# Five scan buffers, single absolute-value buffers and new due times in a one-core Mamba, attention and feed-forward block

## The reference

```python
x = x + selective_scan(layernorm(x))      # 16 states, scan over the 512 tokens
x = x + ffn(layernorm(x))                 # fp4-quantised, 256 -> 704 -> 256, gate and up
x = x + linear_attention(layernorm(x))    # 16 heads of 16, running sums over tokens
x = x + ffn(layernorm(x))                 # the same feed-forward again
```

## Time and profile before

| what | value |
|---|---|
| median of 3 runs | 3002.07 us (3000.82 to 3004.05) |
| the profiled execution: its time | 3002.07 us |
| its span in the profile | 3000.3 us |
| mean granted clock of TensorE | 0.921 |
| busy: PE, DVE, ACT, POOL | 82%, 79%, 63%, 32% |
| instructions | 40700 |

### The profile page before, as it was taken

One profiled execution on the slowest core, in us unless ns is written; L12 is line 12 of the kernel. 1 busy time (PEld: TensorE's weight loads), 2 busy tenths in 40 slices (PEclk: granted clock), 3 DMA queues, 4 the chain that ended last, 5 costly groups with the idle time before them and its releaser, 6 DMA issues.

```text
span 3000.3 us, 40700 instructions
## 1 busy us (share of the span) xinstructions
PE 2453.8 (82%) x12908; PEld 1396.4 (47%) x12908; DVE 2364.2 (79%) x4136; ACT 1900.8 (63%) x3677; POOL 963.7 (32%) x1632
## 2 busy tenths in 40 slices
PE   3559798887979788797988879798887979879796
PEld 1115354453535445354554535455353545536464
DVE  7776887969788796978879697887969788787744
ACT  4667667585766757576575757658575675846342
POOL 3012332333333232333333233233323323333432
PEclk7669899999999999999999999999999999989898
DMA  3321212112121211212112121211212121121000
GB/s 74 109 81 53 70 44 72 47 53 67 49 71 46 64 55 47 74 41 78 41 52 73 40 76 43 75 46 52 73 40 75 45 74 46 52 60 40 4 5 9
DMA packets 104434, 165.97 MB, mean 55 GB/s; under 512 B 15442, under 2 KB 34078, under 8 KB 104222
## 3 DMA queue, kind: packets, MB, share of 16 engines
q1 hardware_dynamic: 104222, 163.37, 19.8%
HBM read 146.55 MB, written 16.78 MB: 54 GB/s over the span
## 4 chain that ended last, share of the span: by engine, by line
PE 40%; DVE 36%; ACT 17%; issue 5%; POOL 2%; DMA 1%; SPq 0%; DVEq 0%; ACTq 0%; POOLq 0%
PE bank L916 10%; PE bank L899 9%; DVE scan_bufs L1187 7%; DVE scan_bufs L1197 4%; PE acc_y L864 4%; PE bank L956 3%; DVE rounding L1055 2%; ACT p_xT L615 2%; DVE f_h_max L1082 2%; ACT masked_scores L667 2%; PE bank L896 2%; PE bank L937 2%; DVE f_h L1057 2%; PE bank L909 1%; ACT scan_bufs L605 1%
## 5 line engine op out<-in xcount | busy, mean ns | idle before, releaser
L1187 DVE TENSOR_TENSOR_SCAN scan_bufs<-scan_bufs,inp_bank 128x512 f32<-128x512 f32 x512 | 617.2, 1205 | 24.4 <-ACT scan_bufs L607 12.9
L899 PE MATMUL bank<-w_gu,f_xqT 128*128 128x512 f32 x1024 | 495.8, 629 | 52.1 <-ACT f_xqT L667 23.6
L916 PE MATMUL bank<-w_dn,f_hqT 128*128 128x256 f32 (+1 forms) x1536 | 425.7, 423 | 36.3 <-ACT yT L667 33.6
L864 PE MATMUL acc_y<-scan_bufs,sel_y 128*32 128x512 f32 x1024 | 301.1, 674 | 127.9 <-DVE scan_bufs L1197 127.8
L605 ACT ACTIVATE scan_bufs<-scan_bufs,a_rows 128x512 f32<-128x512 f32 x512 | 365.4, 714 | 9.2 <-DMA scan_bufs<-dt_copy 8.7
L916 PEld LDWEIGHTS bank<-w_dn,f_hqT 128*128 128x128 f32 (+1 forms) x1536 | 297.0, 207 | 155.9 <-issue 78.9
L1197 DVE TENSOR_TENSOR scan_bufs<-scan_bufs,c_bank 128x512 f32<-128x512 f32 x512 | 343.6, 671 | 11.8 <-issue 0.2
L899 PEld LDWEIGHTS bank<-w_gu,f_xqT 128*128 128x128 f32 x1024 | 197.3, 201 | 310.0 <-issue 263.9
L607 ACT ACTIVATE scan_bufs<-scan_bufs 128x512 f32<-128x512 f32 x512 | 322.6, 630 | 16.2
L527 POOL TENSOR_TENSOR f_h<-f_h,f_h_inv 128x704 f32<-128x704 f32 x128 | 178.2, 1392 | 368.0 <-DVE f_h_inv L1086 368.0
L527 POOL TENSOR_TENSOR f_h<-f_h,f_h_scale 128x704 f32<-128x704 f32 x128 | 178.3, 1393 | 278.2 <-DVE f_h L1057 278.1
(11 more groups left out here) (194 smaller groups left out, 4642.7 us busy)
## 6 DMA issues: line engine op xcount, KB each, us to landing
scan_bufs<-dt_copy SPq DMA_DIRECT2D x512, 256.0 KB, 3.6
xp<-L_attn_a_x SPq DMA_DIRECT2D x16, 512.0 KB, 4.1
dt_copy<-dt SPq DMA_DIRECT2D x32, 256.0 KB, 2.0
out<-x SPq DMA_DIRECT2D x64, 128.0 KB, 2.0
w_attn<-L_attn_b_W_attn SPq DMA_DIRECT2D x1, 768.0 KB
scan_bufs<-L_ffn_w_gate SPq DMA_DIRECT2D x1, 704.0 KB
scan_bufs<-L_ffn_w_up SPq DMA_DIRECT2D x1, 704.0 KB
masked_scores<-L_ffn_w_down SPq DMA_DIRECT2D x1, 704.0 KB
```

What stands on the lines that cost most here:

```text
L864: last = nc.tensor.matmul(acc_y[32 * j:32 * j + 32, :], sel_y[:, q, :], bar[slot][:, h, :], start=(q == 0), stop=(q == 3), tile_position=( ...
L899: last = nc.tensor.matmul(to[:, :], f.xqT[:, k, :], w_gu[:, k, g, lo:hi], start=(k == 0), stop=(k == DH - 1))
L916: last = nc.tensor.matmul(to[:, 0:D], f.hqT[0:n, k, :], w_dn[0:n, k, :], start=(k == 0), stop=(k == FK - 1))
L1187: nc.vector.tensor_tensor_scan(half, half, inp[:, :], 0.0, ALU.mult, ALU.add)\
```

## The change

It adds a fifth slot to `scan_bufs`. It gives each feed-forward one buffer in place of two for the absolute values of x and of h, and ACT therefore waits for the rounding of the tile before in place of the one two tiles before. And it changes many of the beats in `TIMES`, and one in `PARTS_AT`.

```diff
-SLOTS = 4
+SLOTS = 5
...
-"S": (48.95, 16, 2), "Y": (65.0, 1, 2)
+"S": (48.75, 16, 2), "Y": (65, 1, 2)
...
     "sp": {
-        ("P", "load"): 2.25, ("P", "keep0"): 24.5, ("P", "keep1"): 26.7, ("D", "spread"): -3.55, ("R2", "down"): 13.9,
+        ("P", "load"): 1.35, ("P", "keep0"): 24.4, ("P", "keep1"): 26.6, ("D", "spread"): -3.05, ("R2", "down"): 14.8,
...
     "pe": {
-        ("P", "xT0"): 7.35, ("P", "xT1"): 10.1, ("P", "u0"): 10.3, ("P", "u1"): 14.6, ("P", "low"): 15.4,
-        ("P", "B"): 16.6, ("P", "C"): 32.6, ("P", "dt0"): 20.5, ("P", "dt1"): 24.5, ("P", "G"): 30.6,
+        ("P", "xT0"): 7.35, ("P", "xT1"): 8.3, ("P", "u0"): 10.5, ("P", "u1"): 14.55, ("P", "low"): 15.4,
+        ("P", "B"): 16.6, ("P", "C"): 32.4, ("P", "dt0"): 20.5, ("P", "dt1"): 23.5, ("P", "G"): 30.6,
...
-        ("R1", "a_s0"): 16.2, ("R1", "a_s1"): 17.35, ("R1", "a_sum"): 18.3, ("R1", "a_flip"): 18.8,
-        ("R1", "a_turn_y"): 20.3, ("R1", "a_proj"): 21.0, ("R2", "turn_x"): 5.0, ("R2", "up0"): 5.8,
-        ("R2", "up1"): 7.7, ("R2", "turn_h"): 10.7, ("R2", "down"): 11.6,
+        ("R1", "a_s0"): 16.2, ("R1", "a_s1"): 17.35, ("R1", "a_sum"): 18.1, ("R1", "a_flip"): 18.8,
+        ("R1", "a_turn_y"): 20.3, ("R1", "a_proj"): 21.0, ("R2", "turn_x"): 5.3, ("R2", "up0"): 5.8,
+        ("R2", "up1"): 7.8, ("R2", "turn_h"): 10.7, ("R2", "down"): 12.3,
...
-                self.x_abs = [sb(f"{name}_x_abs{i}", [P, D], BF16) for i in range(2)]
-                self.h_abs = [sb(f"{name}_h_abs{i}", [P, F], BF16) for i in range(2)]
+                self.x_abs = sb(f"{name}_x_abs", [P, D], BF16)
+                self.h_abs = sb(f"{name}_h_abs", [P, F], BF16)
...
-                    if not first(b, t - 1):
-                        act.wait_ge(f.x_rounded, upto(b, TILES, t - 2))
-                    nc.scalar.activation(f.x_abs[r][:, :], f.x[r][:, :], ACT.Abs, scale=ROUNDER_PER)\
+                    if not first(b, t):
+                        act.wait_ge(f.x_rounded, upto(b, TILES, t - 1))
+                    nc.scalar.activation(f.x_abs[:, :], f.x[r][:, :], ACT.Abs, scale=ROUNDER_PER)\
```

More of the change, by code:

```diff
@@ L33 @@
 BEATS = 2 * NS
-SLOTS = 4
+SLOTS = 5
 HALVES = NS * DH
 N_SETUP_POOL = 26
-PARTS_AT = {"P": (0, 0, 1), "M": (32, 1, 32), "D": (32, 2, 16), "G": (32, 2, 16), "S": (48.95, 16, 2), "Y": (65.0, 1, 2), "R1": (66, 3, 4), "R2": (95.7, 7, 4)}
+PARTS_AT = {"P": (0, 0, 1), "M": (32, 1, 32), "D": (32, 2, 16), "G": (32, 2, 16), "S": (48.75, 16, 2), "Y": (65, 1, 2), "R1": (66, 3, 4), "R2": (95.7, 7, 4)}
 LAST_AT = {"R1": (66, 3), "R2": (88, 3)}
@@ L688, in ffn @@
                     act.wait_ge(f.h_scaled, upto(b, TILES, t))
-                    if not first(b, t - 1):
-                        act.wait_ge(f.h_rounded, upto(b, TILES, t - 2))
-                    nc.scalar.activation(f.h_abs[r][:, :], f.h[r][:, :], ACT.Abs, scale=ROUNDER_PER)\
+                    if not first(b, t):
+                        act.wait_ge(f.h_rounded, upto(b, TILES, t - 1))
+                    nc.scalar.activation(f.h_abs[:, :], f.h[r][:, :], ACT.Abs, scale=ROUNDER_PER)\
                         .then_inc(f.abs_ready[1], 1)
@@ L1225, in ffn @@
                     dve.wait_ge(f.abs_ready[0], upto(b, TILES, t))
-                    round_mag(ch, (f.x[r][:, :], rounding[:, 0:D]), f.x_abs[r][:, :], f.x_rounded, b, t)
+                    round_mag(ch, (f.x[r][:, :], rounding[:, 0:D]), f.x_abs[:, :], f.x_rounded, b, t)
                 elif s in ("up0", "up1"):
@@ L1255, in ffn @@
                     dve.wait_ge(f.abs_ready[1], upto(b, TILES, t))
-                    round_mag(ch, (f.h[r][:, :], rounding[:, :]), f.h_abs[r][:, :], f.h_rounded, b, t)
+                    round_mag(ch, (f.h[r][:, :], rounding[:, :]), f.h_abs[:, :], f.h_rounded, b, t)
             def attention(b, par, t, s):
```

## The result

The changed kernel takes 3073.86 us, the median of 4 runs (3072.65 to 3074.98), against 3001.45 us for the kernel before beside it: ratio 1.0241, 95% interval 1.0223 to 1.0259. It is slower, as forecast, but by 72 us and not by 42, and outside the range. The profiled execution has a span of 3072.1 us.

What follows compares the result with a forecast made beforehand. No engine is full; the interlocking of the engines' hand-written orders bounds the kernel, delays of the leading engine being paid in full. 3002.1 + 42.9 (13 batches) + 4.4 (tail) - 5 (slot) = 3044.4 us; range 3000 to 3070.

Steps and rivals of the forecast that it cites:

- Steps 1 to 6: Six reorderings in one batch, from its boundary to a_qkv of tile 2: +0.65, +0.8, 2.3 (including both), -0.7, +0.2, +1.2 us.
- the norm: ScalarE does P norm ahead of the tanh of R2 up0, so VectorE gets the tanh later: +0.8 us a batch.
- turn_h ahead of u0: TensorE does R2 turn_h before P u0 and resumes 2.5 us later, of which 2.3 a batch are let through.
- a_sum ahead: a_sum of tiles 0, 1 and 2 goes before a_qkv of the next tile: 0.2 + 1.2 + 0.3 us a batch.
- 2.3 - 0.7 + 0.2 + 1.2 + 0.3 = 3.3 us: Whole batch: late turn_h, R1 up1 and turn_h of tile 2 earlier, then three a_sum moves; 42.9 us for 13 batches.
- step 7: a_sum of tile 2 before a_qkv of tile 3, R2 down of tile 2 behind dt1 on VectorE: +0.3 us, between 0 and 0.9.
- the short third kind of batch: One batch in three keeps the full clock at u0; none expected to afterwards, 0.6 us on average, in the high end only.
- The tail: Last stage, R2 of the last batch: TensorE's up0 ahead of down delays VectorE on three tiles, +4.4 us in all.
- The slot: Fifth scan-buffer slot removes ScalarE's wait for copies in the first batch: -5 us, between 0 and 6.5.
- A: Rival: the moves are hidden in VectorE's 32 us without work per batch; time 3002 us, chance 0.08.
- C: Rival: the single absolute-value buffer binds in the feed-forwards, 52 us on top of the forecast; time 3096 us, chance 0.04.
- B: Rival: R1 down of tile 3 keeps the full clock, gaining 2.25 us a batch; time 2973 us, chance 0.16.

Runs made afterwards that it cites:

- d1: Kernel before with one needless addition on VectorE per batch, 0.77 us longer: ratio 1.0050, batch 177.5 us.
- d3: Kernel before with two needless additions on VectorE per batch, 1.55 us longer: ratio 1.0109, batch 178.5 us, in threes.
- d2: Kernel before with three needless additions on VectorE per batch, 2.47 us longer: ratio 1.0212, batch 180.6 us.
- h1_fill: Kernel before with needless TensorE products in three waits (ahead of P u0, a_turn_y of tile 0, a_turn of tile 2): ratio 1.0201, batch 180.6 us.
- g4_fill: Kernel before with needless TensorE products in four waits, those of h1_fill and a_flip of tile 1: ratio 0.9982, batch 175.7 us.
- h2_fill: Changed kernel with needless TensorE products in seven long waits: ratio to the kernel before 1.0182, batch 179.7 us.
- e4_down: Kernel before with only R2 down later and the C projection ahead of it: ratio 1.0034, batch 177.5 us.
- e3_asum: Kernel before with only a_sum of a tile ahead of a_qkv of the next: ratio 1.0074, batch 177.5 us.
- e5: Kernel before with only R2 turn_h of tile 0 ahead of P u0 on TensorE: ratio 1.0047, batch 177.6 us.
- e1: Kernel before with five scan slots and single absolute-value buffers, all beats as before: ratio 1.0000, batch 176.5 us.
- e2: Changed kernel's beats with the old four scan slots and double absolute-value buffers: ratio to the kernel before 1.0242, batch 181.0 us.
- g5_fill: Kernel before with needless TensorE products in five waits, those of g4_fill and R2 turn_x of tile 0: ratio 0.9981, batch 175.9 us.
- f34_two_undone: Changed kernel with the a_sum moves and the R2 down and C moves undone: ratio to the kernel before 1.0345, batch 184.3 us.

## Why the prediction was right in direction and wrong in size

- **Steps 1 to 6 as places**: right, within 0.3 us in the changed trace, up to the last logarithm, 2.95 late for a predicted 3.0. As prices of a whole batch they were not: the norm alone costs 0.2, turn_h ahead of u0 alone 1.2, a_sum ahead alone 1.1 in place of 1.7.
- **The step that failed** is the sum: "2.3 - 0.7 + 0.2 + 1.2 + 0.3 = 3.3 us", added to a batch of 176.4 with the clock left as it was. The measured 4.9 close as 2.95 up to the logarithm, 1.1 behind it (step 7, next point), 0.45 for the short third kind of batch, which is gone (the batch read here was one of 176.85, the mean was 176.4), and 0.4 for two long batches. Of the 1.6 missed, 0.8 are step 7, 0.45 the short batch, which I had written down as 0.6 and put into the range and not into the sum, and 0.4 the long ones. The premise that a delay in the leading engine "is paid in full", and no more, fell too: a pure delay costs 1.4 to 1.7 times itself (d1, d3, d2). Two parts of that are shown: the short third batch goes with the smallest delay, 0.4 us of the 1.1, and low stretches grow, the one at u0 to twice its length with 2.47 us, 1.2 us.
- **Step 7**, "something between 0 and 0.9; I take 0.3": it measured 1.1 in this batch (2.95 late at the logarithm, 4.05 at the batch's end against 176.85 us), counted from last read to last read; from first scan to first scan 0.5 of the loss lies behind the logarithm. The stretch at 1.2 GHz from 1552 to 1562 falls on it: R2 down of tile 2 takes 5.17 us, and a_qkv of tile 3, now also behind a_sum of tile 2, starts 155.45 us behind the last read, before at 146.11. h1_fill against g4_fill shows that such a stretch, some 10 us earlier in the order, costs up to 4.9 us, and h2_fill's own batches that it costs some 3 us there. In the changed kernel itself its share of the 1.1 stays open: e4_down, with only 3.41 us at 1.2 GHz there, takes 28.5 us behind the logarithm too.
- **The batches together**: 63.4 us for 42.9: 4.5 a batch in the steady state, 0.4 on average from the two long batches, whose cause I did not find. "13 equal batches" was misread to begin with: those of the kernel before come in threes.
- **The tail**: +4.4 for a measured +8.2 behind the last scan, and +4.8 between the last batch's first and last scan, which my sum left out altogether: 13.0 together. The exchange itself was sized about right, though misread: PE does up0 of a tile ahead of the down of the tile two before, and for two tiles, not three. DVE's last three L1237 lie 19.17 and 16.78 us apart, before 15.78 and 14.73, 5.4 us more for my 4.4, and 1.2 come back behind them. The other 8.9 of the 13.0 us lie ahead, between the last batch's first scan and the first of these three, and my sum had nothing for them. e3_asum alone is 10.5 us late there, so they go with a_sum ahead of a_qkv in the last batch; e4_down is 3.6 early there. In e3_asum PE waits twice for q_par, 3.5 us together, ahead of the scores, which it did not before; that a_sum no longer stands between a_qkv and the scores would explain it, and the rest of the 10 us was not traced.
- **The slot**: the start came out at -4.8 for my -5 by luck. 4.0 come with the beats alone; the buffers alone are worth 2.4 there and nothing in the time.
- **Rivals**: A (hidden) and C (single buffer) are refuted, by e3 to e5 and by e1 and e2. B fell: R1 down of tile 3 kept its low clock (5.34 us), and g5_fill shows that with every low stretch gone a batch is 1.4 us shorter, not 2.25.

The changed tail's last two tiles on DVE, then the last of the kernel before, whose 2957.39 is in the earlier trace rows:

```profile
3028.36 0.69 DVE L1237 SCALAR_TENSOR_TENSOR f_h<-f_tanh,bank 128x512 f32<-128x512 f32 x1 [0.21 <-DVE x L1215]
...
3044.50 0.42 DVE L1215 TENSOR_TENSOR x<-bank,x 128x256 f32<-128x256 f32 x1 [4.46 <-PE bank L916]
3045.14 0.69 DVE L1237 SCALAR_TENSOR_TENSOR f_h<-f_tanh,bank 128x512 f32<-128x512 f32 x1 [0.21 <-DVE x L1215]
```

```profile
2972.12 0.69 DVE L1237 SCALAR_TENSOR_TENSOR f_h<-f_tanh,bank 128x512 f32<-128x512 f32 x1 [2.00 <-ACT f_tanh L703]
```

In the changed kernel the 0.21 us ahead of up0 are a wait for the down in front of it, and that one waited 4.46 us for PE.

**What stays open** is why a batch prefers certain lengths. Eleven kernels have steady batches of 177.5, 180.9 or 184.3 us. A feedback between the point in a batch where PE goes idle and the point where the clock falls would do that: it is argued from the traces, not shown. h1_fill shows that the clock is in it, and h2_fill, whose long batches come out at 180.9 with a logarithm 2.4 us sooner, that a gain can be taken back to the same length. The kernels in threes fit as well: three batches take 529.1 us before and 535.9 in d3_late, and three of 177.5 take 532.5, which is 3.4 us from either.

## What to carry to other kernels

A delay read off a timeline gave the place well and the price only roughly here, where the stages repeat and TensorE's clock moves with them: measure the exchange rate once, with a pure delay of known length, before adding terms up. Where single edits give identical times, don't subtract their prices; look for what makes the periods equal, and never assume that undoing half of a bad change helps. Walk through the last batch and the tail with the same care as through a steady batch, since a product that hides a latency in one may be all that hides it in the other. And when one profile holds repetitions of two lengths, compare these with one another: h2_fill's own batches gave the price that no pair of kernels did.

## What the runs showed of the hardware

- The stretches at 1.2 GHz last 3.41, 6.82, 10.24 or 13.65 us in the windows of d1_late, d2_late, h1_fill and f34_two_undone above. The three steady lengths of a batch, 177.5, 180.9 and 184.3 us, are 3.4 us apart too; why is open.
- The clock fell at 1552.1 us in the changed kernel although PE was busy 2.40 of the 3.32 us ahead, with score products on 32 rows and transposes. The Trainium skill, "TensorE: Matmul & The Clock Gate", What's actually happening, says that the clock follows how busy the array has been recently, at 1.2 GHz when idle. The waits of 3.15 us at u0 agree; the fall at 1552.1 came with TensorE at work most of the time.
- Needless products in the waits hold it up, 0.99 over four batches of g5_fill, for 0.3% of the time at best. A new low stretch can follow at a later wait: filling three waits cost 2.0% (h1_fill), filling the fourth brought it back to -0.2% (g4_fill).
